# A graph network on one core: gathers released five selection pairs later, and the last layer's gathers signalled by quarters

## The reference

```
h = (x @ W)                                   # 4 heads of 32
e = leaky_relu(a_src[src] + a_dst[dst])
ex = exp(e - segment_max(e, dst)[dst])
alpha = ex / (segment_sum(ex, dst)[dst] + 1e-16)
out = segment_sum(h[src] * alpha, dst) + bias # then relu; twice
z = layernorm(x + out)
msgs = z[dst] @ Wd + z[src] @ Ws + edge_weight * ww + bm
agg = segment_max(msgs, dst)                  # 0 where a node has no edge
z = layernorm(z + relu(z @ W1a + agg @ W1b + b1) @ W2 + b2)
```

## Time and profile before

| | us |
|---|---|
| three runs, median (lowest to highest) | 8574.75 (8574.27 to 8578.88) |
| the profiled execution | 8585.75 |
| its span, first to last instruction | 8583.6 |
| mean granted TensorE clock | 0.583 of full speed |

### The profile page before, as it was taken

How to read it: one execution, slowest core, us unless ns; L and a number is a source line. 1 busy time by engine, 2 the same in 40 slices (tenths; PEclk the granted TensorE clock), 3 DMA queues, 4 the chain that set the end, 5 groups by cost and what they waited for, 6 DMA issues and landing times.

```text
span 8583.6 us, 135722 instructions
## 1 busy us (share of the span) xinstructions
PE 5437.7 (63%) x24591; PEld 5012.9 (58%) x24591; DVE 4120.3 (48%) x11945; ACT 4686.1 (55%) x10649; POOL 4889.6 (57%) x5170
## 2 busy tenths in 40 slices
PE   6777777677776677777777677634554445454556
PEld 6666666666666566666666666534444444444445
DVE  3444444444446344444444444645444444444557
ACT  4666566566566566656566556644444434344447
POOL 5566666566663655666666656345555555555562
PEclk6555555555556555555555555557677676667779
DMA  7333333333342433334333333354554444454554
GB/s 198 92 97 96 94 97 94 91 98 95 93 98 62 128 93 97 94 93 100 95 95 98 92 92 100 87 149 128 129 129 127 127 127 126 126 126 127 130 140 135
DMA packets 820560, 943.20 MB, mean 110 GB/s; under 512 B 185720, under 2 KB 549570, under 8 KB 819522
## 3 DMA queue, kind: packets, MB, share of 16 engines
q1 hardware_dynamic: 658962, 595.34, 25.2%
q0 software_dynamic: 160256, 335.36, 17.6%
q10 hardware_dynamic: 432, 2.45, 0.1%
HBM read 883.19 MB, written 49.44 MB: 109 GB/s over the span
## 4 chain that ended last, share of the span: by engine, by line
PE 15%; issue 12%; DVE 11%; another core or an unknown queue 11%; DVEq 2%; ACT 1%; DMA 0%; SPq 0%; POOL 0%; ACTq 0%
PE bS L806 7%; DVE acc L1399 4%; PE bA L771 3%; DVE ch L1638 2%; DVE bA L1632 2%; PE bA L694 1%; PE bE L694 1%; DVEq L1399 1%; PE bM L694 1%; PE bM L806 1%; PE bE L806 1%; DVEq L1265 0%; DVEq L1385 0%; DVE acc L1394 0%
## 5 line engine op out<-in xcount | busy, mean ns | idle before, releaser
L673 POOL DMA_INDIRECT G<-table,idx x3328 | 3140.6, 944 | 2057.2 <-issue 891.9
L806 PE MATMUL bS<-G,S 128*128 x8816 | 2187.9, 411 | 911.5 <-issue 383.1
L806 PEld LDWEIGHTS bS<-G,S 128*128 128x128 f32 x8816 | 1880.4, 298 | 1031.2 <-issue 1021.2
L673 POOL DMA_INDIRECT G<-ztable,idx x1664 | 1569.7, 943 | 1165.6 <-issue 455.7
L1399 DVE TENSOR_TENSOR acc<-acc,bS 128x136 f32 (+1 forms) x4408 | 1282.4, 291 | 1804.2 <-remote 801.8
L771 PEld LDWEIGHTS bA<-adst,st 128*128 128x128 f32 x7872 | 1797.3, 331 | 455.4 <-issue 453.4
L771 PE MATMUL bA<-adst,st 128*128 x7872 | 1748.2, 344 | 354.5 <-issue 281.7
L1054 ACT ACTIVATE S<-iota_row,nd 128x128 f32<-128x128 f32 x5904 | 1864.1, 387 | 48.5 <-issue 42.4
L1040 ACT ACTIVATE st<-xr,neg_p 128x512 f32<-128x512 f32 x984 | 701.4, 713 | 1513.5 <-remote 848.1
L1058 ACT ACTIVATE S<-S,one_col 128x512 f32<-128x512 f32 x1476 | 1065.2, 722 | 55.6 <-issue 7.3
L1044 ACT ACTIVATE st<-st,one_col 128x512 f32<-128x512 f32 x984 | 710.0, 722 | 31.9
(11 more groups left out here) (217 smaller groups left out, 4410.3 us busy)
## 6 DMA issues: line engine op xcount, KB each, us to landing
xr<-d_drel SPq DMA_DIRECT2D x984, 256.0 KB
xr<-in_ew SPq DMA_DIRECT2D x312, 256.0 KB
st<-d_neg SPq DMA_DIRECT2D x312, 256.0 KB
G<-table,idx POOLq DMA_INDIRECT x3328
G<-ztable,idx POOLq DMA_INDIRECT x1664
isend<-in_ew SPq DMA_DIRECT2D x104, 256.0 KB
isend<-d_neg SPq DMA_DIRECT2D x104, 256.0 KB
table<-G SPq DMA_DIRECT2D x48, 264.0 KB
```

Source lines behind the costliest of these rows:

```text
L673: pool.indirect_dma_start(G[:, r, c, 0:width], None, from_table, bass.IndirectOffsetOnAxis(ap=idx[:, r, c:c + 1], axis=0)).then_inc(gather ...
L806: mm = pe.matmul(bank_of(l, u, r, k)[:, j * w:(j + 1) * w], S[:, onehots(r, i), s, :], Gf[:, bass.ds(chunk_at[0][s], w)], start=True, stop ...
```

## The change

GpSimd's wait before each two gathers asks for a count of `sel_done` that is five pairs higher; the line serves all three layers. In the last layer the gathers raise one semaphore for each quarter of a batch (8 chunks, 128) instead of one for the batch; TensorE waits for a quarter before each second step, and SP's index load waits for all four.

```diff
+        pieces = [sems(f"piece{r}_", 4) for r in range(RING)]
...
             def idx_load(l, b, r, it):
                 done = 512 * (landed(l, r, it) - 1)
-                if due(done):
+                if l == 2 and (not isinstance(b, int) or b >= RING):
+                    for m in range(4):
+                        sp.wait_ge(pieces[r][m], 128 * it)
+                        sp.nop(nofuse=True)
+                elif due(done):
                     sp.wait_ge(gathered[r], done)
                     sp.nop(nofuse=True)
...
                         if c % 2 == 0 and (not isinstance(b, int) or b >= RING):
-                            pool.wait_ge(sel_done, 2 * quad(l, b - 2, 0) + c // 2 - 3)
+                            pool.wait_ge(sel_done, 2 * quad(l, b - 2, 0) + c // 2 + 2)
...
-                                                bass.IndirectOffsetOnAxis(ap=idx[:, r, c:c + 1], axis=0)).then_inc(gathered[r], 16)
+                                                bass.IndirectOffsetOnAxis(ap=idx[:, r, c:c + 1], axis=0)).then_inc(gathered[r] if l < 2 else pieces[r][c // 8], 16)
...
                 def turn_v(b, r, it, s):
                     n = NS * b + s
-                    if s == 0:
-                        pe.wait_ge(gathered[r], 512 * landed(l, r, it))
+                    if s % 2 == 0:
+                        pe.wait_ge(pieces[r][s // 2], 128 * (it + 1))
+                        pe.nop(nofuse=True)
```

## The result

| | before | changed |
|---|---|---|
| median of 4 runs each, us | 8576.81 (8574.27 to 8584.07) | 8512.32 (8497.89 to 8513.92) |
| span of the profiled execution, us | 8583.6 | 8511.8 |
| mean granted TensorE clock | 0.583 | 0.589 |

The ratio is 0.992, with a 95% interval of 0.9905 to 0.9935: 64.5 us less, where the prediction's sum had 6. The range held the time and the sign was right, but the gain is ten times the forecast one, and both terms that the sum put at nothing turned out large, with opposite signs.

A forecast was written before the change was run, and what follows sets the result against it. A batch was taken to last as long as GpSimd's 32 gathers and its stops. Later wait 0, quarters -7, added waits +1 made -6 us: 8574.75 to 8568.8, said as 8568.5, range 8455 to 8722.

The forecast's parts named there:

- the hold: In a run of n gathers, TensorE's results stop arriving after 5 to 6 us, for about 1.25 n - 3 us.
- Rival 4: Stalls come from code loading: the later wait gives 0, the last layer's quarters the whole 29.5 us; 8546, chance 0.07.
- part 2: Start of the last layer: signalling gathers by quarters lets TensorE begin 29.5 us earlier, saving 7 us (2.6 to 11.2).
- first case: Whole kernel: the summed forecast of -6 us, 8568.5 us, own range 8535 to 8600, chance 0.50.
- rivals 1 and 2: Attention layers: the hold falls on the serial chain, 8719 (chance 0.25), or runs of gathers even out, 8460 (chance 0.18).
- its own signs: Attention layers: a batch within 0.4 us of 49.9 us, and 1346 gathers in 2100 us kept within 1%.
- Part 1 in the last layer: Later wait there: still four to five runs a batch, so 0 us a batch, bounds ±1 over 47 batches.
- Part 1 in the attention layers: Later wait there: again four runs a batch, so 0 us a batch, bounds -2.3 and +3.3 over 94 batches.
- Rival 1: Attention layers: four more gathers put the hold on exponents and scales, 1.6 us a batch; 8719, at most 8879, chance 0.25.
- The walk: Attention layers, through TensorE's pairs k0 to k17: four runs, stops before k4, k10, k15, k1; batch 49.4 us, or 51.
- Rival 3: Last layer's start: quarters do nothing, TensorE is held from the start; 8574, inside the first case, no own chance given.
- Part 3: Last layer: the added waits of TensorE and SP cost 1 us, between 0 and 92 us.

The follow-up runs named there:

- pauses: last_only plus three clears of a scratch tile after every fourth gather of the last layer; chip B, without the hold: ratio 1.0695.
- pauses_again: The same kernel as pauses, on chip D, which has the hold: 8491.6 us, ratio 0.9832.
- half: last_only with every second gather of the last layer left out, so its result isn't computed; chip B, without the hold: ratio 0.9327.
- half_again: The same kernel as half, on chip C, which has the hold: 7524.6 us, ratio 0.8774.
- shift_only: Changed kernel with the quarters undone; the wait stays five pairs later in all three layers; chip A: 8569.9 us, ratio 0.9946.
- last_only: Changed kernel with the attention layers' wait put back; later wait and quarters in the last layer alone; chip A: 8519.5 us, ratio 0.9879.
- quarters_only: Changed kernel with GpSimd's wait put back in all layers, quarters kept; chip A: 8622.1 us, ratio 0.9989.
- ring: last_only, attention layers waiting before every eighth gather, last layer's batches 2 to 4 also released pair by pair; chip B, without the hold: ratio 0.9974.
- spaced: last_only plus one clear of a scratch tile after every gather of the last layer; chip B, without the hold: ratio 1.0207.

## Why the prediction was right, and where it wasn't

**What bounds the kernel: right.** A batch is 32 gathers and GpSimd's stops, and the stops come with the hold. pauses against pauses_again shows it, half against half_again too, and so does the chip that has none: 39.9 us a batch. Rival 4, code loading, is out: it would have given 29.5 us at the last layer's start, where 1.7 came.

**The sign was luck.** The forecast was faster because of part 2's -7, which came as -1.7; what made the kernel faster was put at nothing. The time also lies outside the first case's own range (8535 to 8600) and inside the whole one only because that was widened for rivals 1 and 2, neither of which came. By its own signs the prediction failed as well: the attention layers' batch is 50.8 us, 0.9 off 49.9 where 0.4 was allowed, and 1323 gathers instead of 1346 are 1.7% off, not 1%.

**Part 1 in the last layer: the step that failed.** It said 0 us a batch with bounds of ±1, "each free window of TensorE still releases about four pairs, so four to five runs a batch". There are five runs a batch as before, but the stops aren't alike. I priced the stops by their number, at the size that they have in the attention layers (2.1 to 3.2 us); in the last layer's trace one stop in five, the one ahead of a batch's first gather, was 6.1 us on average, and mostly 8 where it stood behind a run of four that began some 2.3 us after a long one. Measured: -3.4 us a batch, 145 us between the result's two traces and 93 us on chip A. The row was there to be read: the last layer's batch was 3 us longer than the attention layers' with the same number of gathers, and I didn't ask which stop held them. That the later wait removes the long stops is shown, in every trace that has it in the last layer; that the short run's place makes them is read from the timelines, and no run moved it by itself.

**Part 1 in the attention layers: 0 forecast, +86 us measured** (+35 on chip A). Of it 22.5 us are the last batch of each layer, which I had used as evidence without seeing that later gathers would fill it, and 3.7 us lie before the change begins. Of the rest, 25.5 are the four batches ahead of those, at 3.2 us each, and 34 are 0.4 us a batch, inside the bounds. Rival 1 had the sign and the wrong place: from exponents to scales it is 5.1 us on average, 5.4 before. What grew is the way from the logits to the exponents, 20.7 to 25.6 us, while the scaling of the values lost 2.4. The walk's stops (before k4, k10, k15 and k1) came true: of 88 batches all stop before k1, 75 before k4, 84 before k9 or k10 and 80 before k14, k15 or k16; 68 do all four. What was mis-sized is the stop before k1, 3.3 us where k14's was 2.0. The prediction had named that case ("with the third stop and the rest before k1 longer, 51") and then took 0.

**Part 2: -7 forecast, -1.7 measured,** under the lower end of 2.6. "A group of four takes 22.4/2 = 11.2 us" was wrong: from scan to scan a group takes 22.4 us or 44.8 in that run once its first ones are done, and the groups gained at its front are lost at its end. Before as after, VectorE has made four scans when the run ends. Rival 3 comes nearest. *Part 3,* the added waits, was forecast at 1 us and shows nowhere clearly: shift_only without them and last_only with them have last layers of 2576.8 and 2577.9 us from first to last gather.

**The end,** 10.7 us, wasn't in the sum. quarters_only has 190.5 us after the last gather's start, shift_only 178.1: it comes with the wait. The likely reason, which no run tests, is that the last gathers are tied to later pairs and less is left behind them.

So the sum that gave -6 should have read +86 - 145 - 1.7 - 10.7 = -71, the difference of the two traces; the medians differ by 64.5. Two large terms of opposite sign had both been taken as nothing. Their sizes vary by chip: the loss in the attention layers is 86 us in the result, 81 on C and 35 on A (of it 48, 48 and 47 in the last five batches of the layers), and what the last layer gains from the wait is 145 us and 93.

**Open:** what the hold is, and why one chip of four has none. Whether the changed kernel differs from the kernel before without the hold wasn't measured; ring, which contains the change in the last layer, gave 0.9974 there. A rest shorter than 1.44 us, or after more than four gathers, and rests in the attention layers weren't tried; GpSimd's own time would be 32 × 1.25 + 4 × (1.44 - 0.30) = 44.6 us a batch with a rest after every eight, if that is enough: an estimate from the pitch of 1.25 us, of which 0.30 is the gap that a rest replaces. spaced, a short clear in every gap, ran only on the chip without the hold, so whether a slower pitch alone keeps the hold away is open too.

## What to carry to other kernels

Stops of an engine are not alike: before pricing a shift by their number, list them by the run that precedes them, stage by stage, and look for the long one. A change to one line that serves several stages has as many prices as stages; on chip A the wait moved in all three layers gave 59 us (shift_only), and moved in the last alone it gave 109 (last_only, with the quarters). And when a stall follows an engine's own bursts, a short rest placed by hand can cost no more than the stalls; here it shortened what follows the last burst by 32 us.

## What the runs showed of the hardware

On three of four chips, while GpSimd issues a row of indirect DMAs every 1.25 us, the other engines' results stop arriving from some 5 to 6 us into the row until, mostly, 2.3 to 3.5 us after it (read from which pairs release GpSimd and when the others go on). On one chip the same code has no such stall, and the kernel takes 6871 us instead of 8575 to 8637. On chip D a rest of 1.44 us after every four indirect DMAs kept it away. In a row of 72, VectorE's scans came 22.4 and 44.8 us apart. TensorE's granted clock isn't the difference: 0.50 in the attention layers on both kinds of chip.
